# A state-space stage rewritten from its first norm to its scan: taps, one joint projection, ranks counted by products

## The reference

```python
scores = jnp.squeeze(gelu(xn @ r_w1 + r_b1) @ r_w2 + r_b2, -1)
_, topk_idx = jax.lax.top_k(scores, 32)
# the 96 others, in order, are u:
xi, z = jnp.split(u @ in_w, 2, axis=-1)                  # 256 channels each
xc = silu(conv_b + sum(pad(xi)[:, j:j + L] * conv_w[:, j] for j in range(4)))
proj = xc @ xproj_w                                       # 8 + 16 + 16 columns: dt, B, C
delta = softplus(dtp @ dt_w + dt_b)
# h_t = exp(delta A) h + delta xc B ;  y = h C + xc Dp    (a scan over 96 tokens)
y = (y * silu(z)) @ out_w
```

## Time and profile before

| what | us |
|---|---|
| median of 3 runs (461.05 to 463.77) | 461.35 |
| the profiled execution | 461.0 |
| its span, first to last instruction | 459.2 |
| TensorE busy in the span | 403.7 (88%) |
| VectorE busy | 286.7 (62%) |
| ScalarE busy | 230.3 (50%) |
| GpSimd busy | 138.8 (30%) |
| mean granted clock of TensorE | 0.978 |

### The profile page before, as it was taken

One profiled execution on the slowest core, in us unless ns is written; L12 is line 12 of the kernel. 1 busy time (PEld: TensorE's weight loads), 2 busy tenths in 40 slices (PEclk: granted clock), 3 DMA queues, 4 the chain that ended last, 5 costly groups with the idle time before them and its releaser, 6 DMA issues.

```text
span 459.2 us, 9900 instructions
## 1 busy us (share of the span) xinstructions
PE 403.7 (88%) x3974; PEld 263.9 (57%) x3974; DVE 286.7 (62%) x704; ACT 230.3 (50%) x428; POOL 138.8 (30%) x117
## 2 busy tenths in 40 slices
PE   3788998999987979998689999989999799999992
PEld 2445666457753835654456666654667456666662
DVE  5796966756656556245499988763466544444546
ACT  1425563745744045768599999414555542222220
POOL 5839552300123025130088998410001200000001
PEclk9999999999999997999799999999999999999997
DMA  7320000000000000002112322053000000000001
GB/s 183 81 68 1 3 4 2 1 3 3 4 2 0 1 0 1 1 1 57 51 62 79 126 90 91 2 165 110 3 1 5 2 0 1 0 0 2 0 1 46
DMA packets 17023, 14.42 MB, mean 31 GB/s; under 512 B 6435, under 2 KB 14147, under 8 KB 16979
## 3 DMA queue, kind: packets, MB, share of 16 engines
q1 hardware_dynamic: 15680, 13.09, 9.7%
q10 hardware_dynamic: 1299, 0.71, 0.6%
HBM read 13.22 MB, written 0.57 MB: 30 GB/s over the span
## 4 chain that ended last, share of the span: by engine, by line
PE 67%; DVE 14%; ACT 11%; issue 4%; DMA 1%; POOL 1%; ACTq 0%; POOLq 0%; DVEq 0%
PE PS L1669 7%; PE PS L1730 6%; PE PS L1734 6%; PE PS L1366 6%; PE PS L1761 6%; PE PS L1298 4%; PE PS L1345 4%; ACT att L632 4%; PE PS L1656 3%; PE PS L1312 3%; PE PS L1381 3%; PE PS L1585 2%; ACT att L789 2%; PE PS L1428 2%; ACT outT L643 2%
## 5 line engine op out<-in xcount | busy, mean ns | idle before, releaser
L632 ACT ACTIVATE att<-PS 77x512 f32<-77x512 f32 (+1 forms) x96 | 51.7, 591 | 45.9 <-PE PS L1369 45.9
L898 DVE TENSOR_REDUCE mxp<-PS 128x4 f32<-128x308 f32 (+1 forms) x96 | 48.0, 536 | 32.1 <-PE PS L1345 32.1
L495 POOL TENSOR_TENSOR rstd<-ve,neg_half 128x1 f32<-128x1 f32 x24 | 13.3, 556 | 120.3 <-DVE ve L960 120.3
L824 ACT ACTIVATE kM<-PS 128x512 f32<-128x512 f32 x32 | 19.1, 597 | 56.3 <-PE PS L1730 56.3
L1195 DVE TENSOR_TENSOR_SCAN big<-big,PS 128x768 f32<-128x768 f32 x22 | 38.2, 1749 | 7.3 <-PE PS L1656 7.3
L1298 PE MATMUL PS<-negsel,identb 128*128 128x512 bf16 x152 | 37.6, 392 | 2.1 <-DVE big L1000 1.6
L1251 DVE TENSOR_TENSOR big<-kM,PS 128x512 f32<-128x512 f32 x32 | 21.9, 687 | 27.3 <-PE PS L1734 26.0
L489 POOL TENSOR_TENSOR rstd<-ve,neg_half 128x4 f32<-128x4 f32 x6 | 6.2, 1031 | 104.0 <-DVE ve L854 104.0
L1730 PE MATMUL PS<-xT,V 128*128 128x512 f32 x64 | 32.9, 595 | 0.8 <-DVE xT L1239 0.8
L1734 PE MATMUL PS<-xT,V 128*128 128x512 f32 x64 | 32.7, 592 | 0.0
L1761 PEld LDWEIGHTS PS<-big 128*128 128x128 f32 x256 | 29.7, 192 | 3.3 <-issue 3.3
(11 more groups left out here) (349 smaller groups left out, 889.5 us busy)
## 6 DMA issues: line engine op xcount, KB each, us to landing
kM<-Cdram SPq DMA_DIRECT2D x6, 384.0 KB, 3.2
XH<-Cdram SPq DMA_DIRECT2D x5, 384.0 KB, 3.6
xT<-Cdram SPq DMA_DIRECT2D x5, 384.0 KB, 3.4
V<-in_L_ffn_Wg SPq DMA_DIRECT2D x1, 1024.0 KB, 5.6
V<-in_L_ffn_Wu SPq DMA_DIRECT2D x1, 1024.0 KB, 8.2
convw<-in_L_attn_conv_w SPq DMA_DIRECT2D x1, 512.0 KB
out_x<-X SPq DMA_DIRECT2D x2, 256.0 KB, 2.3
ctxN<-in_ctx ACTq DMA_DIRECT2D x1, 308.0 KB
```

The source lines that it names most:

```text
L632: A_(PT[0:nk, i % 2, g], bank4(at.bank("exp", i, g), nk), ACT.Exp, scale=at.scale)\
L898: V_.tensor_reduce(mxp[:, b % 3, g, 0:J], PS[:, at.bank("max", b, g), 0:J * nk].rearrange("p (j k) -> p j k", j=J), axis=AX.X, op=ALU.max) ...
```

## The change

- The in-projection runs on the unpermuted tokens, all 512 columns for each sequence b (`XI.b`), placed between the steps of the ranking. Perm is applied to the projected values, 96 columns at a time, into banks 4 to 7.
- The convolution is no product any more: ScalarE writes the last tap with the bias, VectorE adds the three others from PSUM to it, ScalarE applies silu.
- One product by xproj gives dt, B and C (40 rows); delta is a product of dt_w, with dt_b as a row against a row of ones. B is had by turning that projection, C is rows 24 to 39 of it. GpSimd's multiplied weights, Wdt and the masked q are gone.
- Ranks: VectorE compares (bf16 zeros and ones), TensorE sums them by products with a column of ones. Perm comes in two halves.
- W5T, k5 and v5 go ahead of xnT; V5 is cleared by GpSimd right after the second attention.
- Exp, softplus and du are done by halves of the tokens (c) instead of the channels (h), relu by VectorE from PSUM. The small attention's softmax is not divided before its product: its output and its sums are products (256 of 32 columns), divided afterwards, ahead of du's transposes in TensorE's queue.
- `y_start` goes behind `inputs(0)`; ScalarE scales du's first half before the first decay.

The core of the diff, by engine; first the loads, SyncE and GpSimd:

```diff
-                (convw[:], a["L1_attn_conv_w"].rearrange("(o n) c -> o n c", o=1).to_broadcast([128, DIN, DC])),
+                (convw[:], a["L1_attn_conv_w"].rearrange("(h p) c -> p h c", p=128)),
...
-        dring.wait_copied(sp, "C.1")
+        sp.wait_ge(event("proj_copied"), 2)
...
-        loaded(pool, "ssm")
-        for j in range(DC):
-            ins = P_.tensor_tensor(out=convin[:, j, :], in0=inw4[:, 0:DIN], in1=convw[:, :, j], op=ALU.mult)
-        ins.then_inc(event("ssm_weights"), 1)
+        value_ones(V5[:])
+        step(P_.memset(colmask[:], 0.0))
+        affine(colmask[:].rearrange("p j (g i d) -> p j g i d", g=G, i=J), ALU.not_equal, [[1, J], [0, G], [-1, J], [0, HD]], 0)\
+            .then_inc(event("colmask"), 1)
+
+        pool.wait_ge(event("colmask"), 1)
+        pool.wait_ge(at2.pv_done, B)
+        P_.memset(att[32:64, 0:W768], 1.0).then_inc(event("proj_ones"), 1)
+        pool.wait_ge(event("proj_ones"), 1)
...
-        pool.wait_ge(event("equal_scores"), 1)
-        P_.tensor_tensor(out=eq, in0=eq, in1=before[:].rearrange("p (o t) -> p o t", o=1).to_broadcast([128, B, T]),
-                         op=ALU.mult).then_inc(event("equal_earlier"), 1)
-        value_ones(V5[:])
...
+        loaded(pool, "ssm")
+        pool.wait_ge(event("xc_ready"), 2 * NH)
```

ScalarE:

```diff
+        table(ACT.Gelu_apprx_tanh)
+        copy_out("W5T", W5T[:], bank4)
+        masked("k5.0", lambda j: kM5[:, j, 0:HB, :], bank_ctx, headmask, None)
         for c in range(2):
             copy_out(f"xnT.{c}", half(xT, c), bank4, scale=lnwb4[:, 0:1], bias=lnwb4[:, 1:2])
         for c in range(2):
             copy_out(f"router.{c}", half(hrT, c), lambda i: bank4(i, D // 2), ACT.Gelu_apprx_tanh, bias=rb1[:])
+
+        def token_in(b):
+            copy_out(f"XI.{b}", XI[:, b, :], bank_full, ACT.Copy)
+
+        token_in(0)
...
+        table(ACT.Silu)
...
+        for n in range(2 * NH):
+            c, h = n // NH, n % NH
+            act.wait_ge(event("xi_ready"), n + 1)
+            A_(acc[:, h, c, :], PS[:, 4 + n, 0:W384], ACT.Identity, scale=convw[:, h, DC - 1:DC], bias=convb[:, h:h + 1])\
+                .then_inc(event("tap"), 1)
+        act.wait_ge(event("chosen_ready"), 1)
+        A_(chosenT[:].rearrange("p b k -> p (b k)"), PS[:, 0, 0:B * KSEL], ACT.Identity, scale=lnwb4[:, 0:1], bias=lnwb4[:, 1:2])\
+            .then_inc(event("chosen_copied"), 1)
+
+        def conv_silu(c):
+            for h in range(NH):
+                act.wait_ge(event("conv"), c * NH * (DC - 1) + NH * (DC - 2) + h + 1)
+                A_(xc[:, h, c * W384:(c + 1) * W384], acc[:, h, c, :], ACT.Silu).then_inc(event("xc_ready"), 1)
+
+        conv_silu(0)
...
+        conv_silu(1)
+        act.wait_ge(event("proj_ones"), 1)
+        for c in range(2):
+            act.wait_ge(event("proj_ready"), c + 1)
+            A_(projsb[0:NPROJ, c * W384:(c + 1) * W384], PS[0:NPROJ, 4 + c, 0:W384], ACT.Copy).then_inc(event("proj_copied"), 1)
+        for c in range(2):
+            w = slice(c * W384, (c + 1) * W384)
+            act.wait_ge(event("proj_ready"), 2 + NH * (c + 1))
+            sized = act_step.then(A_(sp_exp[:, :, w], PS[:, 6 - 2 * c:8 - 2 * c, 0:W384], ACT.Abs))
+            if c == 0:
+                A_(Aneg[:], Alog[:], ACT.Exp).then_inc(event("a_exp"), 1)
+            act.wait_ge(act_step.sem, sized)
+            A_(sp_exp[:, :, w], sp_exp[:, :, w], ACT.Exp, scale=-1.0).then_inc(event("sp_exp"), 1)
+        act.wait_ge(event("small_attention"), 2)
+        A_(Pa[:], Pa[:], ACT.Exp, scale=1 / math.sqrt(HD)).then_inc(event("sp_exp"), 1)
+        for c in range(2):
+            act.wait_ge(event("turned"), c + 2)
+            A_(half(PermT, c), bank4(1 + c), ACT.Copy).then_inc(event("z_copied"), 1)
+
+        def z_copy(n, h, c, bank):
+            act.wait_ge(event("z_ready"), n)
+            A_(zs[:, h, c * W384:(c + 1) * W384], PS[:, bank, 0:W384], ACT.Copy).then_inc(event("z_copied"), 1)
+
+        z_copy(1, 0, 1, 3)
+        z_copy(2, 1, 1, 1)
+        for c in range(2):
+            w = slice(c * W384, (c + 1) * W384)
+            act.wait_ge(event("sp_exp"), c + 1)
+            A_(sp_log[:, :, w], sp_exp[:, :, w], ACT.Ln, bias=1.0).then_inc(event("sp_log"), 1)
...
+        z_copy(3, 0, 0, 6)
+        z_copy(4, 1, 0, 7)
...
+        act.wait_ge(event("duT_ready"), 1)
+        A_(duT[:, 0:NK // 2, :], PSflat[:, 4 * 512:4 * 512 + W768].rearrange("p (k d) -> p k d", k=NK // 2), ACT.Identity)\
+            .then_inc(event("duT0_copied"), 1)
+        act.wait_ge(event("duT0_copied"), 1)
+        act.wait_ge(event("BT_copied"), 1)
+        scale(0, range(NK // 2))
         decay(0)
-        act.wait_ge(event("duT_ready"), 1)
-        A_(duT[:, :, 0:128], PSflat[:, 4 * 512:4 * 512 + W768].rearrange("p (k d) -> p k d", k=NK), ACT.Identity)\
-            .then_inc(event("duT0_copied"), 1)
+        act.wait_ge(event("duT1_copied"), 1)
+        scale(0, range(NK // 2, NK))
         decay(1)
-        scale(0)
+        scale(1, range(NK))
```

VectorE:

```diff
-        V_.tensor_tensor(eq, Srow, wide(scol[:], [128, B, T]), ALU.is_equal).then_inc(event("equal_scores"), 1)
-        step(V_.tensor_tensor(gt, Srow, wide(scol[:], [128, B, T]), ALU.is_gt))
-        step(V_.tensor_reduce(rank[:], gt, axis=AX.X, op=ALU.add))
-
-        dve.wait_ge(event("equal_earlier"), 1)
-        step(V_.tensor_reduce(ties[:], eq, axis=AX.X, op=ALU.add))
-        step(V_.tensor_tensor(rank[:], rank[:], ties[:], ALU.add))
-        V_.tensor_scalar(unsel[:], rank[:], float(KSEL), None, ALU.is_ge).then_inc(event("unsel"), 1)
-        V_.tensor_scalar(sel[:], rank[:], float(KSEL), None, ALU.is_lt)
+        V_.tensor_tensor(lower, Srow, wide(scol[:], [128, B, T]), ALU.is_lt)
+        for b in range(B):
+            V_.scalar_tensor_tensor(equal[:, b, :], Srow[:, b, :], scol[:, b:b + 1], after[:], ALU.is_equal, ALU.mult)\
+                .then_inc(event("compared"), 1)
+        i = take("rank")
+        V_.tensor_scalar(unsel[:], PS[:, i, 0:B], float(KSEL), None, ALU.is_ge).then_inc(event("unsel"), 1)
+        V_.tensor_scalar(sel[:], PS[:, i, 0:B], float(KSEL), None, ALU.is_lt).then_inc(dring.copied, 1)
...
+            V_.tensor_tensor(half(Perm, c), colnum[:].rearrange("p (o t) -> p o t", o=1).to_broadcast([128, HB, T]),
+                             wide(pos[:, c * HB:(c + 1) * HB], [128, HB, T]), ALU.is_equal).then_inc(event("perm"), 1)
...
+        n = 0
+        for c in range(2):
+            for j in range(DC - 2, -1, -1):
+                for h in range(NH):
+                    if j == DC - 2:
+                        dve.wait_ge(event("tap"), NH * c + h + 1)
+                    else:
+                        dve.wait_ge(event("conv"), n - NH + 1)
+                    late = DC - 1 - j
+                    a_ = acc[:, h, c, :].rearrange("p (b t) -> p b t", b=HB)[:, :, late:TS]
+                    x_ = PS[:, 4 + NH * c + h, 0:W384].rearrange("p (b t) -> p b t", b=HB)[:, :, 0:TS - late]
+                    V_.scalar_tensor_tensor(a_, x_, convw[:, h, j:j + 1], a_, ALU.mult, ALU.add).then_inc(event("conv"), 1)
+                    n += 1
+
+        dve.wait_ge(event("chosen_ready"), 4)
+        dve.wait_ge(event("colmask"), 1)
+        V_.tensor_tensor(vaM, PS[:, 3, 0:2 * D].rearrange("p (n o d) -> p n o d", n=2, o=1).to_broadcast([128, 2, J, D]),
+                         colmask[:].rearrange("p (o j) d -> p o j d", o=1).to_broadcast([128, 2, J, D]), ALU.mult)\
+            .then_inc(event("small_attention"), 1)
...
+        remainders(0)
+        dve.wait_ge(event("sp_exp"), 3)
+        V_.transpose(PaT.rearrange("p n k -> p (n k)"), Pa[:].rearrange("p n k -> p (n k)")).then_inc(event("small_attention"), 1)
+        remainders(1)
+        for c in range(2):
+            w = slice(c * W384, (c + 1) * W384)
+            dve.wait_ge(event("sp_log"), c + 1)
+            dve.wait_ge(event("relu_added"), c + 1)
+            V_.tensor_tensor(delta[:, :, w], sp_log[:, :, w], delta[:, :, w], ALU.add).then_inc(event("delta_ready"), 1)
+            dve.wait_ge(event("delta_ready"), c + 1)
+            V_.tensor_tensor(du[:, :, w], delta[:, :, w], xc[:, :, w], ALU.mult).then_inc(event("du_ready"), 1)
...
+        dve.wait_ge(event("oa_ready"), 1)
+        outs, sums = (PS[:, 0:4, 64 * k:64 * k + 64].rearrange("p c (n q) -> p c n q", n=2) for k in range(2))
+        step(V_.reciprocal(rsa[:], sums))
+        step(V_.tensor_tensor(rsa[:], outs, rsa[:], ALU.mult))
+        V_.tensor_scalar(oaT.rearrange("p n (c q) -> p c n q", c=4), rsa[:], bv4[:], None, ALU.add).then_inc(event("oaT_ready"), 1)
```

TensorE:

```diff
+        loaded(pe, "l5")
+        transposes("W5T", [W5[:, k, :] for k in range(4)], 128, 128)
+        aring.wait_copied(pe, "W5T")
+        product(aring, "k5.0", W5T[:, 1, :], half(ctxT, 0), cols=HB * NC)
+        for c in range(2):
+            row_products(dring, f"v5.{c}", [ctxT[:, b, :] for b in range(c * HB, (c + 1) * HB)], W5T[:, 2, :], NC)
```

(69 more changed lines are left out.)

367 lines of the change are left out of this document (124 added, 243 removed).

## The result

| what | before | after |
|---|---|---|
| median, us (lowest to highest) | 463.36 (461.05 to 465.55) | 460.96 (458.70 to 462.63) |
| after against before | | 0.9942, interval 0.9927 to 0.9957 |
| the profiled execution, us | 461.0 | 462.63 |
| its span, us | 459.2 | 460.8 |
| mean granted clock | 0.978 | 0.953 |

The change makes the kernel 0.6% faster, 2.7 us at the ratio: within 1%, and outside the forecast's range of 448 to 458.5. The forecast was a gain of 9.5 us. The two profiled executions are a poor pair for the total, because before's is its fastest and after's its slowest, so the traces are compared stretch by stretch.

The account below looks back on a forecast made before the run. Bound: a chain of waits, 66.4 us with no engine full, then a full scan. Scan 12.0 us earlier, less 0.7 handovers and 1.8 memset, gains 9.5: 461.0 becomes 451.5 in the profile, 451.8 median; range 448 to 458.5.

Parts of the forecast that it names:

- first scaled copy: ScalarE's first scale of the scan, behind du's transposes and copy: starts at 211.6 us, against 226.03 before.
- second scan: Start of the scan: `y_start` between the inputs of h 0 and h 1 holds it until 219.5 us.
- 512 instructions at 12.5 ns: Small attention's output on TensorE, ahead of du's transposes: priced from L1631's 64 instructions, 6.4 us, until 209.8.
- The rival of 25 ns: Small attention's output: 512 instructions spaced like L1597's 64, 12.8 us instead of 6.4, total 458.2; chance 0.17.
- The lower clock: Rival: z, small products, du's transposes and `y_start` at 1.2 GHz cost 3 to 5 us more, total 456; chance 0.10.
- The memset: Ahead of the stage, near 138 us: GpSimd's 2.65 us clearing of V5 holds VectorE's last tensor_scalar of X; 1.8 us lost.
- not met: Rival: VectorE gets in ahead of GpSimd's memset of V5, so 1.8 us comes back, total 450.0; chance 0.05.
- The scan as long as before: Sign to look for in the changed kernel: the scan stage itself takes as long as before.
- the place of `y_start`: Between the inputs of h 0 and h 1: three products of 0.98 us; lead 12.0 instead of 12.8.
- The comparisons and taps: VectorE: eight comparisons at 0.28 us, twelve taps at 0.55; rival of 0.34 and 0.69 gives 454.5, chance 0.08.
- The lower end of the range: 448 us: all short bounds together, 450.0 less 0.7 and 1.3 of taps and comparisons.
- Slower: Rival: small attention's output at 35 ns an instruction takes 17.9 us, total 463.3; decides from 31 ns; chance 0.05.

Follow-up runs that it names:

- The experiment with `y_start`: Both repairs, plus `y_start` ahead of the inputs of h 0 and masking ahead of VectorE's copy of du's second half: 447.38 us, in a second set 448.08.
- both repairs: Changed kernel with V5's memset behind the third norm's powers and the small attention's tail as before (64 instructions): 448.29 us, again 448.93.

## Why the prediction was wrong

Faster by over 1% had a chance of 0.76, within 1% had 0.20; it came within 1%. Point by point, on the clock of before (the rows of after less 4.15):

| step | forecast | measured |
|---|---|---|
| first comparison begins | 172.7 | 172.4 |
| eight fused comparisons, each | 0.28 | 0.27 |
| a tap on VectorE | 0.55 | 0.52 |
| the 16 permuting products | 3.7 | 3.7 |
| small products begin | 203.4 | 203.65 |
| small products last | 6.4 | 13.2 |
| first scaled copy | 211.6 | 219.2 |
| second scan | 219.5 | 229.7 |
| first half of du ready | 206.3 | 205.0 |
| norm near 139 held by the memset | 1.8 | 1.76 |

- **The failed step** is the term "512 instructions at 12.5 ns". Its price per instruction was right for the 200 that stood ready (2.19 us for the first 201, 11 ns) and even at the lower clock. What failed is the step from 64 instructions in a row to 512: the row of before could not show a supply that runs dry after some 200, and no rival had it. The rival of 25 ns foresaw 12.8 us and came close to 13.2, but by another mechanism, and with other consequences: a uniform price would make half of the products cost 6.6, and it was 4.9.
- **The lower clock** was a rival with 0.10, and its mechanism came true beside the first: z's 24 instructions took 5.43 at 0.50. It hid at first: z took 2.7 more than forecast, and TensorE had come to z 2.4 us earlier than forecast. So the small products began within 0.3 of the forecast by two errors that cancel, which is luck. It cost at the end: `y_start` 5.05 instead of the 2.95 assumed, du's first six transposes 1.49 instead of 0.85, the inputs of h 0 1.51 instead of the 0.82 that the six of h 1 take. Together that covers the 2.9 us left of the miss (9.7 less 6.8). The experiment with `y_start` shows that its place between the inputs turned this into a late second scan. The forecast had seen that place and charged it, at the higher clock.
- **The memset** was charged right, 1.76 for 1.8, and its rival ("not met") is out. Not charged was what follows: a longer wait of TensorE, and 1.1 to 1.5 us of padding at 1.2 GHz. A wait was costed as its own length.
- **The scan as long as before**: 0.9 shorter from its third scan on. The forecast counted neither the reduction at n == 8, which had left it (0.4), nor the place of `y_start` (0.5).
- **The comparisons and taps** were right in size. The sixteen one-column products, taken at 0.1 us each, started 25 ns apart, and the first half of du was ready 1.3 us earlier than forecast; behind the 512 instructions that was worth nothing. The lower end of the range takes off 0.7 and 1.3 "of taps and comparisons"; their bounds give only the 0.7 (12 x 0.05 and 8 x 0.01), and the 1.3 has no working of its own.
- **Slower** (0.04) didn't come; its point was 31 ns an instruction sustained, and 13.2/512 is 26.

The rest of the forecast's sum fits what the kernel with both repairs and `y_start` ahead gains, 463.57 - 448.08 = 15.5 us. By the forecast's own terms the small products cost 3.5 behind du, the memset 1.8 and the place of `y_start` 0.8; with the 9.5 that is 15.6. It is a fit of totals and not a proof of each term, since the lower clock was still paid in that kernel. What stays open is the distance between the medians (2.4) and the two traces (after 1.6 longer, 0.35 without the fall near 18 us): before's other runs are up to 4.5 us longer than its profiled one, and no trace of before shows where. The fall near 18 us (the products there take 3.04 instead of 1.88) shows that such differences between executions of one kernel exist.

## What to carry to other kernels

Count instructions, not only their price: a price read from a short row of small products holds only as long as the instructions are there, so hundreds of tiny products in a row want fewer and wider ones, even if those compute more than is needed. A chain row "issue" of about 2 us between groups of one line, with every engine idle and a packet on the instruction queue for each group, is the mark of it. And a wait on TensorE's path is worth its length plus what the next products take at 1.2 GHz; that second part can come or go with an edit somewhere else, so after each gain look again at the waits behind it.
